# Projection pieces of an attention kernel, two chunks to a step in the narrow query blocks instead of one to a step throughout

## Chip, core and metric

The kernel runs on one NeuronCore of a Trainium2 chip. The metric is the device time of one execution in microseconds (us).

## What is computed

One layer of a language-model tower over 2 x 1024 tokens: a token embedding with two tables (hot and cold rows), causal attention with 16 heads of 32, and a mixture of experts. The part that matters here is the attention:

```python
qkv = jnp.einsum('bsd,od->bso', x, w_project)          # d = 512
q, k, v = (qkv[0], qkv[1], qkv[2])                     # 16 heads of 32
att = jnp.einsum('bhqd,bhkd->bhqk', q, k) / math.sqrt(HEAD_DIM)
att = jnp.where(causal[None, None, :, :], jnp.float32(-1000000000.0), att)
att = jax.nn.softmax(att, axis=-1)
out = jnp.einsum('bhqk,bhkd->bhqd', att, v)
```

## The kernel before

The program has three phases: tokens (until about 115 us of the profile), attention (to about 566 us), and output projection with the mixture of experts (the rest). Each engine runs a list of instructions written out by hand; semaphores tie the lists together.

**Units and steps.** Attention is cut into 8 units (u = 0 to 7), one for a group of 4 heads and one of the 2 sequences. A unit has 32 steps n: query block i = n // 4 (128 queries, i = 0 to 7) and head h = n % 4. Query block i looks at 128 (i + 1) keys, so steps 0 to 15 (blocks 0 to 3, "narrow") have up to 512 keys in one PSUM bank, and steps 16 to 31 (blocks 4 to 7, "wide") have up to 1024 keys in two. A step is a chain over four engines: PE multiplies the scores (L669), DVE finds the row maximum (`row_max`, L808), ACT takes the exponential (`exp`, L766), PE turns the probabilities 128 x 128 at a time (`turn`, L679), and ACT (L751) and DVE (L753) copy the turned banks out. Once in four steps, at n % 4 == 2, PE multiplies a finished block with v (`heads`, L692, and one transpose, L695), ACT copies the sums' inverses (L773) and DVE scales (L823). Scores are issued two steps ahead in the narrow half and one step ahead in the wide half.

**Fills.** While unit u runs, PE also projects q, k and v of unit u + 1 into bank 7. That is 6 fills f: q, k of the first 512 tokens (f = 0, 1), q, k of the second (2, 3), v of the first (4), v of the second (5). A fill is 4 pieces (`fill_piece`). A q or k piece is one chunk k of the 512 input features in three matmuls with high and low parts (L622); a v piece is one token tile in 4 products over all chunks (`value_products`, L635). Within a step, PE's order is scores, turn, fill piece, heads. After the last piece of a fill one engine copies bank 7 out (`fill_evac`): ACT for f = 0, 2 (L539) and 4 (L550), DVE for f = 1, 3 (L543) and 5 (L552). The next fill waits for that copy, since there is one bank for all. Before the change, piece k of fill f is at step 2 + 5 f + k and its copy-out at step 6 + 5 f:

```python
if nxt and 0 <= (n - 2) // 5 < FILLS and (n - 2) % 5 < KC:
    fill_piece(pe, u + 1, 1 - b, (n - 2) // 5, (n - 2) % 5, 16 * (g + 1 + b))
```

Unit 7 has no next unit and no fills.

**What hangs on a fill.** POOL splits the copied q and k into high and low parts (`split_part`, L474, L476), and splits the input rows of the next fills (`split_rows_in`, L497, L501), in the fixed order rows of the first half, q of the first half, rows of the second half, k, q, k (`att_pool`). SP then spreads the parts over partitions in 64 DMAs a unit (`stack_half`, L437): 32 once half of the running unit's scores are issued, and 32 once all are. The first score of a wide block (n = 16, issued in step 15) waits for the second 32.

Of the kernel before, what the change touches and what calls it, by code (L numbers as in the profile page):

```python
# [25 lines left out]
KC = D // P  # L26
# [18 lines left out]
SPLIT0 = 5  # L45
SLOT_RING = 6
SLOT0 = 6
PSLOTS = 2
ROUTED_RING = 8
X_RING = 16  # L50
# [16 lines left out]
def build(nc, a, out):  # L67
    ctx = ExitStack()
    with ctx:
# [312 lines left out]
        HEAD = 16  # L382
# [84 lines left out]
        def split_part(pool, u, side, half):  # L467

            c = slice(half * 512, half * 512 + 512)
            pool.wait_ge(s_fact if side == 0 else s_fdve, HEAD + 3 * u + half + 1)  # L470

            pool.wait_ge((s_high if half else s_low)[(u - 1) % 2], STACKED * ((u - 1) // 2 + 1))
            passed(pool)
            pool.tensor_copy(part_hi[:, side, c], full[:, side, :]).then_inc(s_hi, 1)  # L474
            pool.wait_ge(s_hi, HEAD + 4 * u + 2 * half + side + 1)
            pool.tensor_tensor(part_lo[:, side, c], full[:, side, :],  # L476
                               part_hi[:, side, c].bitcast(F32), ALU.subtract).then_inc(s_lo, 1)

        def split_rows_in(pool, u, half, c, part="both"):

            if u == 1 and half == 0:
                pool.wait_ge(s_xC, 12)
            elif u == 1 and c == 0:
                pool.wait_ge(s_xC, NT)
                pool.wait_ge(s_xpused, 1)
            else:
                v, p = (u, 1) if half else (u - 1, 3)
                if c < KC - 1:
                    pool.wait_ge(s_xpused, 6 * (u - 1) + 3 * half - 3 + c + 1)
                else:  # L490
                    pool.wait_ge(s_fill, HEAD + FILLS * v + p + 1)
# [11 lines left out]
        def split_weights_in(pool, u, c):  # L503

            g = u // 2
            if c == 0:
                pool.wait_ge(s_wq, 16 * (g + 1))
                if u >= 2:

                    pool.wait_ge(s_fill, HEAD + FILLS * (u - 1) + 4)  # L510
            src = w_unit[:, c, 0:2 * P]
            passed(pool)
            pool.tensor_copy(wq_hi[:, c, :], src).then_inc(s_wqhi, 1)
            pool.wait_ge(s_wqhi, 4 * g + c + 1)
            pool.tensor_tensor(wq_lo[:, c, :], src, wq_hi[:, c, :].bitcast(F32), ALU.subtract).then_inc(s_wqlo, 1)
# [15 lines left out]
        def fill_evac(eng, who, u, f, b):  # L531

            src = bank(7)
            n = HEAD + FILLS * u + f + 1
            if f in (0, 2) and who == "act":
                eng.wait_ge(s_fill, n)

# [70 lines left out]
        def fill_piece(pe, u, b, f, k, loads):  # L608

            if k == 0:  # L610

                if f >= 4:
                    pe.wait_ge(s_w, loads)
                copied, count = ((s_fdve, 0), (s_fact, 1), (s_fdve, 1), (s_fact, 2), (s_fdve, 2), (s_fact, 3))[f]
                pe.wait_ge(copied, HEAD + 3 * u + count)
            if f < 4:
                side, half = f % 2, f // 2
# [30 lines left out]
        def att_pe(pe):  # L648
# [49 lines left out]
            def unit(u, b, g, prev, nxt):  # L698

                for n in range(STEPS):  # L700
# [7 lines left out]
                        turn(u, n - 1)  # L708
                    elif prev:
                        turn(u - 1, STEPS - 1)  # L710
                    if nxt and 0 <= (n - 2) // 5 < FILLS and (n - 2) % 5 < KC:
                        fill_piece(pe, u + 1, 1 - b, (n - 2) // 5, (n - 2) % 5, 16 * (g + 1 + b))
                    if n % GH == 2:
                        if n > GH:
                            heads(u, b, n // GH - 1)
# [39 lines left out]
        def att_act(act):  # L755
# [19 lines left out]
            def unit(u, b, prev, nxt):  # L775
                for n in range(STEPS):
# [2 lines left out]
                    elif prev:  # L779
                        copy_turned(act, "act", u - 1, STEPS + n - 2)  # L780
                    exp(u, n)
                    if nxt and (n - 2) % 5 == 4 % 5 and 0 <= (n - 2) // 5 - 0 < FILLS:
                        fill_evac(act, "act", u + 1, (n - 2) // 5 - 0, 1 - b)
                    if n % GH == 3:
                        if n > GH:
                            z_row(u, n // GH - 1)
# [13 lines left out]
        def att_dve(dve):  # L800
# [24 lines left out]
            def unit(u, b, g, pg, nxt):  # L825

                for n in range(STEPS):
                    row_max(u, n)
                    if nxt and (n - 2) % 5 == 4 % 5 and 0 <= (n - 2) // 5 - 0 < FILLS:
                        fill_evac(dve, "dve", u + 1, (n - 2) // 5 - 0, 1 - b)  # L830
                    if n >= 2:
                        copy_turned(dve, "dve", u, n - 2)
                    elif pg is not None:
# [1120 lines left out]
```

## Time and profile before

| | us |
|---|---|
| median of 3 runs (lowest, highest) | 994.73 (993.75, 995.87) |
| the profiled execution's own time | 993.92 |
| its span | 992.1 |
| PE busy in the span | 916.0 (92%) |
| DVE, ACT, POOL busy | 662.9, 596.9, 430.9 |

The span is what the profile shows of one execution. Busy time says how much of the span an engine had an instruction in it; the ends of matmuls are modelled. The windows further below split one unit of the attention by the starts of ACT's exponential at the first step of each block (343.58 us is step 0 of unit 4, 366.04 us its step 16, 400.90 us step 0 of unit 5). All units with fills look alike: from 170.13, 228.10, 285.36, 343.58, 400.90 and 458.17 us the starts of units 1 to 6 are known, and 515.45 us starts unit 7.

### The profile page before, as it was taken

The page shows a single profiled execution, that of the slowest core. Times are in us where ns is not written, and L with a number is a line of the kernel's source. Part 1 is how long each engine was busy: PE and PEld are TensorE (multiplying, and loading weights), DVE is VectorE, ACT ScalarE, POOL GpSimd, SP SyncE. Part 2 cuts the span into 40 slices and gives each one's busy share as a digit, 9 for nine tenths or more (in the row PEclk, how much of TensorE's full clock was granted, in tenths as well). Part 3 has the DMA queues.
Part 4 walks back from the last instruction along what each step waited for, and adds up shares of the span by engine and source line. Part 5 has one row for each costly group of instructions (what it writes and reads, how often), then busy time and mean ns, then how long its engine had stood idle before and what let it go on. Part 6 is the DMA issues. An engine that isn't in the chain of part 4 may idle for free.

```text
span 992.1 us, 21913 instructions
## 1 busy us (share of the span) xinstructions
PE 916.0 (92%) x6923; PEld 701.3 (71%) x6923; DVE 662.9 (67%) x1746; ACT 596.9 (60%) x1306; POOL 430.9 (43%) x460
## 2 busy tenths in 40 slices
PE   6679899999999999999997999899989999999992
PEld 5335678787887878788785788777866666676661
DVE  8885667576666757566666676668866666666660
ACT  7222487777867777786778622221157777777770
POOL 2188554534515255441402126433263377346542
PEclk9699899999999999999999999999999999999997
DMA  6135442424324242432426131441469578746633
GB/s 225 37 93 129 133 118 54 96 57 108 86 65 100 50 117 48 102 82 65 97 46 216 51 119 63 156 195 43 181 214 376 121 134 213 232 86 116 94 53 43
DMA packets 60515, 114.46 MB, mean 115 GB/s; under 512 B 13492, under 2 KB 19636, under 8 KB 58098
## 3 DMA queue, kind: packets, MB, share of 16 engines
q1 hardware_dynamic: 48082, 87.15, 29.4%
q0 software_dynamic: 12320, 25.90, 13.9%
q8 instruction: 58, 0.95, 0.4%
q14 instruction: 55, 0.45, 0.2%
HBM read 53.03 MB, written 25.17 MB: 79 GB/s over the span
## 4 chain that ended last, share of the span: by engine, by line
PE 74%; DVE 10%; issue 5%; SPq 4%; ACT 3%; DMA 2%; POOL 1%; POOLq 0%; DVEq 0%; ACTq 0%
PE psum L1505 13%; PE psum L679 11%; PE psum L1580 8%; PE psum L692 6%; PE psum L669 6%; PE psum L622 6%; PE psum L635 5%; PE psum L644 4%; SPq L437 4%; PE psum L1435 3%; PE psum L1549 2%; PE psum L1527 2%; PE psum L601 1%; PE psum L695 1%; PE psum L1516 1%
## 5 line engine op out<-in xcount | busy, mean ns | idle before, releaser
L766 ACT ACTIVATE probs<-psum,nmax 128x128 f32<-128x128 f32 (+7 forms) x256 | 191.5, 748 | 37.2 <-DVE nmax L808 35.1
L808 DVE CUSTOM_DVE_ANT_0 psum<-psum,mask_row 128x128 f32<-128x128 f32 (+7 forms) x256 | 192.1, 767 | 28.0 <-PE psum L669 26.8
L679 PE MATMUL psum<-ident,probs 128*128 128x128 f32 x1152 | 175.0, 276 | 12.5 <-ACT probs L766 5.5
L679 PEld LDWEIGHTS psum<-ident,probs 128*128 128x128 f32 x1152 | 134.3, 140 | 48.1 <-ACT probs L766 18.0
L751 ACT COPY probsT<-psum 128x512 f32<-128x512 f32 (+3 forms) x256 | 129.6, 506 | 33.5 <-PE psum L679 31.1
L1042 POOL DMA_INDIRECT out<-xnT,slot_out x47 | 82.7, 1759 | 108.1 <-DMA out<-xnT,slot_out 70.3
L669 PE MATMUL psum<-k_low,q_stack 128*128 128x512 f32 (+2 forms) x256 | 105.1, 418 | 6.0 <-ACT probs L766 3.2
L474 POOL CAST part_hi<-full 128x512 fp32r<-128x512 f32 x28 | 17.1, 611 | 206.9 <-ACT full L539 161.1
L823 DVE TENSOR_TENSOR attnT<-psum,z_rows 128x128 f32<-128x128 f32 x64 | 18.7, 292 | 111.7 <-ACT z_rows L773 111.7
L1580 PE MATMUL psum<-w_dn,gated_T 128*128 x188 | 88.6, 593 | 1.0 <-ACT gated_T L1096 1.0
L1361 DVE TENSOR_TENSOR w_lo<-w_gu,w_hi 128x1024 fp32r<-128x1024 f32 x48 | 58.8, 1227 | 42.9 <-ACT w_hi L1125 40.3
L1361 DVE TENSOR_TENSOR ws_lo<-w_gu,ws_hi 128x1024 fp32r<-128x1024 f32 x46 | 56.3, 1227 | 36.0 <-ACT ws_hi L1125 33.8
L692 PE MATMUL psum<-probsT,v_unit 128*32 128x128 f32 x2304 | 76.2, 275 | 0.0
L501 POOL TENSOR_TENSOR x_lo<-xnT,x_hi 128x512 fp32r<-128x512 f32 x56 | 71.8, 1282 | 4.4
L692 PEld LDWEIGHTS psum<-probsT,v_unit 128*32 128x32 f32 x2304 | 59.0, 109 | 15.6 <-ACT probsT L751 7.8
L635 PE MATMUL psum<-w_unit,xnT 128*128 128x128 f32 x512 | 66.8, 275 | 0.2
L753 DVE COPY probsT<-psum 128x128 f32<-128x128 f32 (+3 forms) x128 | 62.2, 486 | 3.7 <-PE psum L679 2.9
L669 PEld LDWEIGHTS psum<-k_low,q_stack 128*128 128x128 f32 x256 | 51.9, 206 | 15.0 <-ACT probs L766 10.6
L635 PEld LDWEIGHTS psum<-w_unit,xnT 128*128 128x128 f32 x512 | 61.7, 192 | 0.6 <-issue 0.6
L1110 ACT ACTIVATE xnT<-psum,slot_w 128x512 f32<-128x512 f32 x47 | 32.4, 690 | 46.9 <-PE psum L1580 44.8
L1125 ACT CAST w_hi<-w_gu 128x1024 fp32r x48 | 50.3, 1049 | 10.8 <-issue 9.0
L622 PE MATMUL psum<-x_lo,wq_hi 128*128 128x512 f32 x112 | 53.8, 480 | 0.0
(262 smaller groups left out, 2144.5 us busy)
## 6 DMA issues: line engine op xcount, KB each, us to landing
w_gu<-in_wgu SPq DMA_DIRECT2D x16, 1024.0 KB, 7.9
q_stack<-part_hi SPq DMA_DIRECT2D x128, 64.0 KB, 2.0
q_stack<-part_lo SPq DMA_DIRECT2D x128, 64.0 KB, 2.0
w_dn<-in_wd SPq DMA_DIRECT2D x16, 512.0 KB, 9.2
out<-acc SPq DMA_DIRECT2D x17, 256.0 KB, 3.1
hot_all<-xn SPq DMA_DIRECT2D x4, 1024.0 KB, 8.0
h_scratch<-hot_all SPq DMA_DIRECT2D x16, 256.0 KB
k_low<-part_hi SPq DMA_DIRECT2D x64, 64.0 KB, 2.0
```

Of the source, the lines that this page charges most:

```text
L622: mm = pe.matmul(bank(7), w[:, k, side * P:(side + 1) * P], x[:, k, :], start=(k == 0 and t == 0), stop=(k == KC - 1 and t == 2), skip_gro ...
L635: mm = pe.matmul(bank(7)[:, k * P:(k + 1) * P], xnT[:, c, t0:t0 + P], w_unit[:, c, 2 * P:3 * P], start=(c == 0), stop=(c == KC - 1))
L669: mm = pe.matmul(dst[:, c0:c1], qs, ks[:, h, 0:c1 - c0], start=True, stop=True)
L679: mm = pe.transpose(bank(4 + m % 2)[:, (j - 4 * k) * P:(j - 4 * k + 1) * P], probs[n % PSLOTS][:, j * P:(j + 1) * P], ident[:, :])
L692: pe.matmul(bank(6)[32 * h:32 * h + 32, 0:P], v_unit[b][:, j, 32 * h:32 * h + 32], probsT[i % 2][:, h, j * P:(j + 1) * P], start=(j == 0), ...
L751: eng.copy(dst, src).then_inc(s_Ca, 1)
L766: act.activation(probs[n % PSLOTS][:, 0:(i + 1) * P], score_bank(n)[:, 0:(i + 1) * P], ACT.Exp, bias=nmax[:, n % 4:n % 4 + 1], scale=-1.0, ...
L808: dve.tensor_tensor_reduce(out=row, in0=row, in1=mask_row[:, (QT - 1 - i) * P:QT * P], scale=1.0, scalar=3.0e38, op0=ALU.add, op1=ALU.min, ...
L1042: pool.indirect_dma_start(out=out, out_offset=bass.IndirectOffsetOnAxis(ap=slot_out[:, j:j + 1], axis=0), in_=y_rows[j % ROUTED_RING], in_ ...
L1361: dve.tensor_tensor(w_lo[j % 2][:, k, :].rearrange("p k n -> p (k n)"), w_gu[:, bass.ds(slot, 1), k, :].rearrange("p o k n -> p (o k n)"), ...
L1505: mm = pe.matmul(bank(2 + p), x[:, p, k * P:(k + 1) * P], w[p][:, k, :], start=(k == 0 and t == 0), stop=(k == KC - 1 and t == 2), skip_gr ...
L1580: mm = pe.matmul(bank(6 + p), gated_T[:, p, k * P:(k + 1) * P], w_dn[:, bass.ds(half, 1), k, :].rearrange("p o n -> p (o n)"), start=(k == 0),
```

## The change

Fills and pieces are the same, but a table places them. The order of the fills becomes q, k, v of the first half, then q, k, v of the second. The first five fills have two pieces to a step, and start at steps 2, 5, 8, 11 and 14; the last v has one piece to a step, at 18 to 21. The copy-outs move to steps 4, 7, 10, 13, 16 and 22. The counts that other engines wait for follow the new order. POOL's and SP's lists are the same.

```diff
+FILL_ORDER = (0, 1, 4, 2, 3, 5)
+FILL_FROM = (2, 5, 8, 11, 14, 18)
+FILL_RATE = (2, 2, 2, 2, 2, 1)
...
-            pool.wait_ge(s_fact if side == 0 else s_fdve, HEAD + 3 * u + half + 1)
+            pool.wait_ge(s_fact if side == 0 else s_fdve, HEAD + 3 * u + (1, 3 - side)[half])
...
-                v, p = (u, 1) if half else (u - 1, 3)
+                v, p = (u, 1) if half else (u - 1, 4)
...
-                    pool.wait_ge(s_fill, HEAD + FILLS * (u - 1) + 4)
+                    pool.wait_ge(s_fill, HEAD + FILLS * (u - 1) + 5)
...
-            n = HEAD + FILLS * u + f + 1
+            n = HEAD + FILLS * u + FILL_ORDER.index(f) + 1
...
-                copied, count = ((s_fdve, 0), (s_fact, 1), (s_fdve, 1), (s_fact, 2), (s_fdve, 2), (s_fact, 3))[f]
+                copied, count = ((s_fdve, 0), (s_fact, 1), (s_fact, 2), (s_fact, 3), (s_fdve, 1), (s_fdve, 2))[f]
...
-                    if nxt and 0 <= (n - 2) // 5 < FILLS and (n - 2) % 5 < KC:
-                        fill_piece(pe, u + 1, 1 - b, (n - 2) // 5, (n - 2) % 5, 16 * (g + 1 + b))
+                    if nxt:
+                        for f, n0, rate in zip(FILL_ORDER, FILL_FROM, FILL_RATE):
+                            for k in range(KC):
+                                if n == n0 + k // rate:
+                                    fill_piece(pe, u + 1, 1 - b, f, k, 16 * (g + 1 + b))
...
-                    if nxt and (n - 2) % 5 == 4 % 5 and 0 <= (n - 2) // 5 - 0 < FILLS:
-                        fill_evac(act, "act", u + 1, (n - 2) // 5 - 0, 1 - b)
+                    if nxt:
+                        for f, n0, rate in zip(FILL_ORDER, FILL_FROM, FILL_RATE):
+                            if n == n0 + KC // rate:
+                                fill_evac(act, "act", u + 1, f, 1 - b)
```

DVE's list changes as ACT's does. Lines of the changed kernel are numbered a few higher (L622 is L625 there, L669 is L672, L679 is L682, L692 is L695).

PE's list in unit 1, steps 10 and 11 (a score L669, turns L679, a fill's chunk L622), before:

```order
L669 MATMUL psum<-k_low,q_stack 128x512
L679 MATMUL psum<-ident,probs 128x128 x3
L622 MATMUL psum<-x_lo,wq_hi 128x512
L622 MATMUL psum<-x_hi,wq_hi 128x512
L622 MATMUL psum<-x_hi,wq_lo 128x512
L692 MATMUL psum<-probsT,v_unit 32x128 x8
L695 MATMUL psum<-ident,z_inv 128x128
L669 MATMUL psum<-k_low,q_stack 128x512
L679 MATMUL psum<-ident,probs 128x128 x3
```

The same two steps of the changed kernel:

```order
L672 MATMUL psum<-k_low,q_stack 128x512
L682 MATMUL psum<-ident,probs 128x128 x3
L695 MATMUL psum<-probsT,v_unit 32x128 x8
L698 MATMUL psum<-ident,z_inv 128x128
L672 MATMUL psum<-k_low,q_stack 128x512
L682 MATMUL psum<-ident,probs 128x128 x3
L625 MATMUL psum<-x_lo,wq_hi 128x512
L625 MATMUL psum<-x_hi,wq_hi 128x512
L625 MATMUL psum<-x_hi,wq_lo 128x512
L625 MATMUL psum<-x_lo,wq_hi 128x512
L625 MATMUL psum<-x_hi,wq_hi 128x512
L625 MATMUL psum<-x_hi,wq_lo 128x512
```

Where one chunk stood in one step and none in the next, none stands now in step 10 and two behind each other in step 11. 

PE's list in unit 1, steps 28 and 29 (block 7, a value piece is L635), before:

```order
L669 MATMUL psum<-k_low,q_stack 128x512
L669 MATMUL psum<-k_high,q_stack 128x512
L679 MATMUL psum<-ident,probs 128x128 x7
L635 MATMUL psum<-w_unit,xnT 128x128 x4
L669 MATMUL psum<-k_low,q_stack 128x512
L669 MATMUL psum<-k_high,q_stack 128x512
L679 MATMUL psum<-ident,probs 128x128 x8
L635 MATMUL psum<-w_unit,xnT 128x128 x4
```

The same place of the changed kernel:

```order
L672 MATMUL psum<-k_low,q_stack 128x512
L672 MATMUL psum<-k_high,q_stack 128x512
L682 MATMUL psum<-ident,probs 128x128 x7
L672 MATMUL psum<-k_low,q_stack 128x512
L672 MATMUL psum<-k_high,q_stack 128x512
L682 MATMUL psum<-ident,probs 128x128 x8
```

Blocks 6 and 7 have no fill pieces left.

ACT's list in unit 1 around step 4 (the copy-out of the first fill is L539, now L542), changed kernel:

```order
L772 ACTIVATE probs,z_sum<-psum,nmax 128x256
L542 ACTIVATE full<-psum 128x512
L757 COPY probsT<-psum 128x128
L772 ACTIVATE probs,z_sum<-psum,nmax 128x256
L757 COPY probsT<-psum 128x256
```

The copy-out stood behind the exponential of step 6 and now stands behind that of step 4.

## Rows read from the trace of the kernel before

**Rows 1.** The page: span, busy time by engine, granted clock, chain by engine

```profile
span 992.1 us, 21913 instructions
...
PE 916.0 (92%) x6923; PEld 701.3 (71%) x6923; DVE 662.9 (67%) x1746; ACT 596.9 (60%) x1306; POOL 430.9 (43%) x460
...
PEclk9699899999999999999999999999999999999997
...
PE 74%; DVE 10%; issue 5%; SPq 4%; ACT 3%; DMA 2%; POOL 1%; POOLq 0%; DVEq 0%; ACTq 0%
```

**Rows 2.** Windows, unit 4: blocks 0 to 7, narrow half, wide half, last step

```profile
core 0: us, PE busy (x) PEld busy (x) DVE busy (x) ACT busy (x) POOL busy (x), PEclk, DMA share, GB/s
343.58:350.07 6.49, 5.94 (x89) 4.80 (x89) 3.14 (x14) 3.20 (x14) 0.00 (x0) 1.00 0.45 102
...
359.79:366.04 6.25, 5.95 (x53) 4.21 (x52) 3.90 (x11) 5.09 (x13) 4.45 (x5) 1.00 0.62 168
366.04:373.60 7.56, 7.44 (x71) 5.70 (x70) 4.44 (x13) 6.13 (x14) 1.89 (x2) 1.00 0.46 105
373.60:381.94 8.34, 8.15 (x93) 6.99 (x91) 6.08 (x17) 6.23 (x13) 5.49 (x8) 1.00 0.42 96
381.94:390.94 9.00, 9.00 (x111) 8.27 (x110) 6.97 (x16) 7.28 (x15) 8.00 (x11) 1.00 0.10 24
390.94:400.90 9.96, 9.96 (x124) 9.08 (x122) 7.41 (x17) 7.33 (x14) 0.00 (x0) 1.00 0.14 40
343.58:366.04 22.46, 21.61 (x213) 16.56 (x213) 13.05 (x48) 16.22 (x54) 11.10 (x12) 1.00 0.49 118
366.04:400.90 34.86, 34.55 (x390) 30.04 (x388) 24.90 (x60) 26.97 (x55) 15.38 (x20) 1.00 0.27 64
397.37:400.90 3.53, 3.53 (x72) 3.04 (x70) 1.89 (x6) 1.96 (x5) 0.00 (x0) 1.00 0.36 107
```

**Rows 3.** Windows, unit 7: narrow half, blocks 4 to 6, block 7's first three steps

```profile
515.45:535.24 19.79, 14.84 (x182) 11.00 (x181) 11.56 (x47) 15.17 (x54) 0.00 (x0) 1.00 0.43 97
535.24:541.61 6.37, 5.29 (x60) 3.83 (x59) 4.35 (x13) 5.64 (x15) 2.74 (x4) 1.00 0.97 375
541.61:549.31 7.70, 6.78 (x73) 4.83 (x74) 6.00 (x16) 6.08 (x13) 7.38 (x9) 1.00 0.84 297
549.31:557.64 8.33, 7.57 (x86) 5.47 (x86) 6.86 (x16) 6.58 (x13) 0.91 (x1) 1.00 0.19 63
557.64:562.95 5.31, 4.86 (x47) 3.34 (x49) 5.28 (x12) 4.97 (x9) 0.00 (x0) 1.00 0.00 0
```

**Rows 4.** Timeline of PE, unit 4, steps 3 to 4 (start, duration, instruction)

```profile
349.00 0.48 PE L622 MATMUL psum<-x_lo,wq_hi 128*128 128x512 f32 x1
...
349.78 0.28 PE L669 MATMUL psum<-k_low,q_stack 128*128 128x256 f32 x1
349.90 0.27 PE L679 MATMUL psum<-ident,probs 128*128 128x128 f32 x1
349.93 0.48 PE L622 MATMUL psum<-x_lo,wq_hi 128*128 128x512 f32 x1
```

**Rows 5.** Chain in order of time: a value piece, and twelve output-projection matmuls (start, length)

```profile
381.29 0.89 PE psum L635 x8
...
582.22 2.87 PE psum L644 x12
```

**Rows 6.** Sources L539 and L543: the copy-outs (min/median/max ns)

```profile
L539 ACT ACTIVATE full<-psum x14: 587/590/604, 121.3 to 481.4; 128x512 f32<-128x512 f32 x14
...
L543 DVE COPY full<-psum x14: 691/692/692, 126.9 to 489.8; 128x512 f32<-128x512 f32 x14
```

**Rows 7.** Timeline of POOL, unit 4: first row split after copy-out, last row split

```profile
352.82 0.61 POOL L474 CAST part_hi<-full 128x512 fp32r<-128x512 f32 x1 [24.41 <-ACT full L539]
...
361.19 1.28 POOL L501 TENSOR_TENSOR x_lo<-xnT,x_hi 128x512 fp32r<-128x512 f32 x1
```

**Rows 8.** Waits, the whole attention: scores that wait for stacks (us, times, longest)

```profile
PE psum L669 <- DMA k_high<-part_lo: 1.4, 2, 0.8
```

More of the change, by code:

```diff
@@ L828, in unit @@
                     row_max(u, n)
-                    if nxt and (n - 2) % 5 == 4 % 5 and 0 <= (n - 2) // 5 - 0 < FILLS:
-                        fill_evac(dve, "dve", u + 1, (n - 2) // 5 - 0, 1 - b)
+                    if nxt:
+                        for f, n0, rate in zip(FILL_ORDER, FILL_FROM, FILL_RATE):
+                            if n == n0 + KC // rate:
+                                fill_evac(dve, "dve", u + 1, f, 1 - b)
                     if n >= 2:
```

## The prediction

> **What bounds the kernel now.** I read the page first. PE is busy 92% of the span and holds 74% of the chain that ended last, at a granted clock that is full nearly everywhere [rows 1]. So the question is where PE has room, and I cut one unit of the attention into windows at ACT's exponentials of each block. In unit 4 PE is busy 21.61 of the 22.46 us of the narrow half and 34.55 of the 34.86 us of the wide half [rows 2]. A unit with fills is PE's from end to end, in both halves. What idle there is lies in block 0, 6.49 less 5.94, so 0.55, and in block 3, 6.25 less 5.95, so 0.30 [rows 2]. Block 0's idle is mostly the hand-over from the last wide block, ahead of the first fill.
>
> Unit 7 has no fills and shows the pace that the rest of a step sets. Its narrow half takes 19.79 us with PE busy 14.84, blocks 4, 5 and 6 take 6.37, 7.70 and 8.33 us with PE busy 5.29, 6.78 and 7.57, and the first three steps of block 7 take 5.31 us [rows 3]. So without fills the narrow half has 5 us of room on PE. But the fills before the change use up that room already.
>
> **What the change does.** No instruction is added or removed: 7 units have 16 q or k pieces and 8 v pieces each, before and after. Before, the narrow half holds 12 q or k pieces (steps 2 to 5, 7 to 10, 12 to 15) and the wide half 4 q or k and 8 v pieces. After, the narrow half holds 16 q or k and 4 v pieces, and the wide half 4 v pieces.
>
> *Price of a piece.* From step 3's chunk to step 4's chunk PE needs 0.93 us, of which the score takes 0.12 (349.78 to 349.90), and the turn that comes before the next chunk about 0.11. A chunk so costs 0.70 [rows 4]. A v piece costs 0.89 [rows 5]. Into the narrow half move 4 x 0.70 + 4 x 0.89 = 6.36 us per unit.
>
> *Do two chunks together cost less than two apart?* PE's rows give a chunk 0.78 us from its own start to the next score [rows 4], while twelve such matmuls in a row take 2.87 us, 0.24 each, so 0.72 for three [rows 5]. But the turn ahead of a chunk starts only 0.03 us before it [rows 4], so that the extra time is the turn's own. I take no gain. The Trainium skill (TensorE: Matmul & The Clock Gate, Step-by-step) says that a matmul alone cannot hide its drain and that in a stream the drain lies beneath the next one. Read as a price for each lone chunk, 0.78 less 0.70 over 8 pairs and 7 units, it would give back 4.5 us of the sum below; the saturated rows speak against it, as lone chunks there have other matmuls on both sides.
>
> *Narrow half.* PE is busy nearly throughout, so the 6.36 us are added. They can fill block 3's idle 0.30 and some of the modelled ends; I take off 0.5. What is new is that the copy-outs fall into short steps. From the end of a fill to the start of the next, PE has in between two steps' scores and turns. After the first fill that is about 0.12 + 0.11 + 0.12 + 0.22 = 0.57 us (two scores of 0.12, three turned tiles of 0.11 [rows 4]), while ACT's copy takes 0.59 [rows 6] and some 0.2 of signalling: 0.25 us of wait. After the other fills at least one block's heads or wider turns lie in between, and I price them at nothing; the heads cover them, and without them each costs up to what the first does. Behind the waiting chunk PE's queue holds the next score and turn, but DVE and ACT have a step in hand then. Narrow: 6.36 - 0.5 + 0.25 = +6.1 us per unit, 22.46 becomes 28.6. The bounds are all idle filled, 6.36 - 0.85 = +5.5, and four copy-outs fully exposed at 0.6 or 0.7 us each [rows 6] and 0.2 of signalling, 6.36 + 3.4 = +9.8.
>
> *Wide half.* PE's work there falls by 6.36 us, but the time cannot fall below the pace of unit 7. Block 6 goes from 9.00 to 8.33 [rows 2, 3]. In block 7 the first three steps go from 6.43 (9.96 less 3.53 [rows 2]) to 5.31 [rows 3], and the last step, where PE is busy all of 3.53 [rows 2], loses nearly its whole piece of 0.89, to 2.7: block 7 8.0. Blocks 4 and 5 take 15.90 us with the pieces of steps 17 to 20, 22 and 23, which are 4 x 0.70 + 2 x 0.89 = 4.58, and 14.07 without [rows 2, 3]; they keep 4 x 0.89 = 3.56. In proportion they would take 15.5, with PE saturated 15.90 - 1.02 = 14.9; I take 15.1, nearer to the saturated end, since PE is busy 15.59 of the 15.90 [rows 2]. Wide: 15.1 + 8.33 + 8.0 = 31.4, so -3.4 us per unit. The bounds are 15.5 + 8.33 + 8.2 = 32.0, -2.8, and unit 7's pace with no cost of the v pieces, 14.07 + 8.33 + 8.0 = 30.4, -4.5.
>
> What is late next in the wide half is ACT and DVE: the 3 us of PE work that do not come back as time turn into PE's waits for the exponential.
>
> *The copy-outs' engines.* ACT is busy 16.22 of 22.46 us in the narrow half and DVE 13.05 [rows 2]. One more copy on each (0.6 and 0.7 us) is hidden in the longer half.
>
> *POOL.* Its list is the same. The last x_lo of the second half ends 361.19 + 1.28 - 352.82 = 9.65 us after POOL takes up q [rows 7]. After the change q is copied out about 0.7 us sooner, and the fill that needs these rows starts at step 11 with two whole fills and their 6.36 us of PE between, some 10 us after that copy; its last chunk is read 1.5 us later still. Hidden, with 1 to 3 us to spare. Were it not, PE's whole list would stand behind that chunk.
>
> *SP.* Its 64 issues per unit stay. The second 32 have to land by step 15, and twice the scores waited for them, 1.4 us in all, 0.8 the longest [rows 8]; with DVE and ACT restarting behind, units 1 and 3 (170.13 to 228.10, 285.36 to 343.58) are 0.7 and 0.9 longer than unit 4. A narrow half that is 6 us longer hides that: -1.7 us in all. The first 32 and the loads of weights have more time than before.
>
> **The sum.** +6.1 - 3.4 = +2.7 us for each of 7 units, 18.9, less 1.7, is +17.2 us. Unit 7 and the phases before and behind stay. Against the profiled execution's own 993.92 us that is 1011.1; the median of the runs lies 0.8 above it, and so I predict 1012. A measurement of this kernel tells about 0.2%, 2 us, from no change.
>
> **Rivals.**
> - *Exposed copy-outs.* One PSUM bank serves all fills, so each of five fills in the narrow half has to be copied out before the next may start, 0.6 to 0.7 us and signalling each time. If the two steps between do not cover it, because a burst of 1.4 us on PE has starved DVE and ACT, all four cost 0.8: +9.8 - 3.1 = +6.7 per unit, +45 us, about 1040; half of that exposed gives 1028. For it: the first one has 0.57 us of PE work to hide 0.8. Against it: PE L622 shows no wait for a copy now, with the same distance of one step, and ACT is idle 28% of the narrow half [rows 2]. Chance 0.10, with what lies above 1024.
> - *The wide half pays everything back* (the other side). Unit 7's blocks 4 and 5 run beside weight loads of 375 and 297 GB/s [rows 3], where the units with fills have 105 and 96 [rows 2]. If unit 7's pace is set by that and not by the chain, the wide half stays PE-bound and loses its 6.36 us; the narrow half gains 5.5: -0.9 x 7 - 1.7 = -8 us, 987. It decides from a wide half below 29.4 us. Against it: block 6 of unit 7 has 63 GB/s and PE idle 0.76 of 8.33 us all the same, and DVE is busy 6.86 of it [rows 3]. Chance 0.04.
> - *A draw.* Wide half at the floor of 30.4 and narrow at +5.5: +1.0 x 7 - 1.7 = +5; with the lone-chunk gain of 4.5 it is nothing, 995. For it: each of the two bounds is possible alone. Chance 0.05.
> - The forecast with its bounds, 1002 to 1024: chance 0.81.
>
> **The numbers.** The range goes from 1002 (the two lower bounds: +5.5 - 4.5 = +1.0 and part of the way to the forecast) to 1024 (a third of the copy-outs' exposure). Slower by over 0.2%: 0.81 + 0.10 and a little of the draw, 0.92. Within 0.2%: 0.04. Faster: 0.04.
>
> **What would show it.** Right: unit 4's successor takes about 60 us from first exponential to first exponential (57.3 before), narrow 28.6 with PE busy nearly all of it, wide 31.4 with PE idle some 2 us or more; block 6 at 8.3; no DMA wait at step 15; the clock at 1.00. Wrong: a wide half below 30 us (rival two), a row of L625 or L638 with idle before it that ends with a copy-out at each fill (rival one), or POOL's x_lo as releaser of PE at step 11 or 12.

## The result and the profile after

The changed kernel takes 1021.43 us (median of 4 runs, 1019.97 to 1022.75) beside 994.81 us before: 1.0257 times as long, with a 95% interval of 1.0238 to 1.0276. It is 26.6 us slower. The profiled execution took 1022.02 us, with a span of 1020.2 us.

The page of the changed kernel, in the lines that answer to [rows 1]:

```profile
span 1020.2 us, 21913 instructions
...
PE 930.3 (91%) x6923; PEld 705.4 (69%) x6923; DVE 659.5 (65%) x1746; ACT 601.0 (59%) x1306; POOL 434.0 (43%) x460
...
PE 73%; DVE 10%; issue 6%; DMA 4%; ACT 3%; SPq 2%; POOL 1%; POOLq 0%; ACTq 0%; DVEq 0%
```

The page hardly differs: the same instructions, the same engine on the chain, 28.1 us more. PE is busy 14.3 us longer with the same 6923 matmuls, so its busy time, with modelled ends, is not a fixed sum of work. Windows tell more. Those of unit 4, cut at the same exponentials as in [rows 2] (blocks 0, 3, 4, 5, 6 and 7, then the narrow and the wide half; columns as there):

```profile
357.60:364.79 7.19, 6.64 (x91) 5.33 (x91) 3.15 (x14) 3.21 (x15) 0.00 (x0) 1.00 0.41 94
...
377.79:385.27 7.48, 7.48 (x63) 6.03 (x62) 3.39 (x10) 5.82 (x14) 1.91 (x2) 1.00 0.47 123
385.27:393.89 8.62, 7.56 (x81) 6.44 (x79) 5.02 (x15) 5.86 (x13) 6.58 (x10) 1.00 0.41 93
393.89:402.55 8.66, 8.20 (x93) 7.03 (x93) 6.88 (x17) 6.39 (x13) 6.91 (x9) 1.00 0.41 94
402.55:410.48 7.93, 7.35 (x86) 5.49 (x86) 6.50 (x16) 6.59 (x13) 0.00 (x0) 1.00 0.19 50
410.48:418.46 7.98, 7.53 (x95) 5.63 (x93) 6.40 (x16) 6.94 (x14) 0.00 (x0) 1.00 0.13 29
357.60:385.27 27.67, 27.00 (x254) 22.15 (x254) 12.90 (x47) 17.89 (x56) 12.95 (x14) 1.00 0.44 104
385.27:418.46 33.19, 30.63 (x349) 24.59 (x347) 24.80 (x61) 25.78 (x53) 13.49 (x18) 1.00 0.29 68
```

The narrow half went from 22.46 to 27.67 us, with PE busy nearly throughout, and the wide half from 34.86 to 33.19 with PE idle 2.56. Blocks 6 and 7, without pieces, fell to 7.93 and 7.98. Block 4 rose from 7.56 to 8.62 and block 5 from 8.34 to 8.66, though block 4 holds about as much fill work as before (two thirds of a chunk and two v pieces, against three chunks) and block 5 one chunk less.

Where PE's idle time in block 4 comes from, in the timeline of the changed kernel (start, duration, instruction, idle before and its releaser):

```profile
385.60 0.39 PE L625 MATMUL psum<-x_hi,wq_lo 128*128 128x512 f32 x1
...
386.02 0.69 DVE L546 COPY full<-psum 128x512 f32<-128x512 f32 x1 [0.78 <-PE psum L625]
...
386.63 0.17 DVE L823 RECIPROCAL z_rec<-z_sum 128x4 f32<-128x4 f32 x1
386.83 0.23 DVE L825 COPY z_inv<-z_rec 128x128 f32<-128x128 f32 x1
386.98 0.82 DVE L816 CUSTOM_DVE_ANT_0 psum<-psum,mask_row 128x640 f32<-128x640 f32 x1
...
387.89 0.80 ACT L772 ACTIVATE probs<-psum,nmax 128x640 f32<-128x640 f32 x1 [0.50 <-DVE nmax L816]
...
388.83 0.50 PE L672 MATMUL psum<-k_low,q_stack 128*128 128x512 f32 x1 [1.06 <-ACT probs L772]
```

The second chunk of step 15 ends, DVE has waited 0.78 us for it, copies k out, inverts the sums and only then takes the row maximum of step 17. The exponential and the score two steps on wait behind it, and PE stands idle for 1.06 us.

Step by step, the 28.1 us between the two spans: unit 0 starts 0.87 later (116.37 for 115.50), units 0 to 6 take 423.90 us for 399.95, which is 23.95 more, and from the start of unit 7 to the end it is 479.93 for 476.65, 3.28 more. Of these 3.28, unit 7 has 1.26: from its first exponential to the end of its last it takes 49.88 us for 48.62. The other 2.0 fall behind it, where the edit touches nothing; over all kernels below that stretch runs from 426.5 to 431.2 us (428.0 before, 430.1 here). Unit 7 has a new wait, in PE's timeline of the changed kernel:

```profile
559.73 0.48 PE L672 MATMUL psum<-k_low,q_stack 128*128 128x512 f32 x1 [1.79 <-DMA k_high<-part_lo]
...
560.92 0.78 PE L672 MATMUL psum<-k_low,q_stack 128*128 128x512 f32 x1
```

and in the windows of its narrow half and its block 4 the granted clock is no longer 1.00:

```profile
540.27:561.79 21.52, 15.35 (x179) 11.46 (x179) 11.79 (x48) 15.18 (x53) 0.00 (x0) 0.96 0.44 98
561.79:569.51 7.72, 7.05 (x66) 5.11 (x64) 5.24 (x15) 6.88 (x17) 4.63 (x6) 0.89 1.02 394
```

The narrow half of unit 7 takes 21.52 us where it took 19.79 [rows 3]. The stacks are issued once all scores of unit 6 are out. Unit 6's last step is now 2.66 instead of 3.53 us [rows 2], so the stacks start about 0.9 us later against unit 7, and unit 7 has no fills that would hide them. The last part of k_high lands 19.32 us after the first exponential of unit 7, before the change 18.11 us after it. That the shorter last step is what makes this difference is argued; no run varied it.

### The profile page after: what moved, and what is told of

The parts are those of the page before. It is cut to its first block, busy times and chain, and to the rows that moved or that the text cites. A ratio compares the mean times of both kernels' runs of the same rounds, so it can differ in the third digit from the quotient of the medians.

```text
span 1020.2 us, 21913 instructions
## 1 busy us (share of the span) xinstructions
PE 930.3 (91%) x6923; PEld 705.4 (69%) x6923; DVE 659.5 (65%) x1746; ACT 601.0 (59%) x1306; POOL 434.0 (43%) x460
## 4 chain that ended last, share of the span: by engine, by line
PE 73%; DVE 10%; issue 6%; DMA 4%; ACT 3%; SPq 2%; POOL 1%; POOLq 0%; ACTq 0%; DVEq 0%
PE psum L682 12%; PE psum L1515 11%; PE psum L625 8%; PE psum L672 7%; PE psum L1590 7%; PE psum L695 7%; PE psum L638 5%; PE psum L647 4%; DMA out<-xnT,slot_out 4%; PE psum L1445 3%; SPq L440 2%; PE psum L1559 2%; PE psum L1537 2%; PE psum L698 2%; DVE oh_lo L1756 1%
## 5 line engine op out<-in xcount | busy, mean ns | idle before, releaser
L816 DVE CUSTOM_DVE_ANT_0 psum<-psum,mask_row 128x128 f32<-128x128 f32 (+7 forms) x256 | 192.1, 767 | 25.7 <-PE psum L672 23.8
L682 PE MATMUL psum<-ident,probs 128*128 128x128 f32 x1152 | 175.2, 278 | 12.1 <-ACT probs L772 4.2
L682 PEld LDWEIGHTS psum<-ident,probs 128*128 128x128 f32 x1152 | 132.7, 141 | 48.9 <-issue 23.3
L672 PE MATMUL psum<-k_low,q_stack 128*128 128x512 f32 (+2 forms) x256 | 108.7, 437 | 18.7 <-ACT probs L772 16.3
L477 POOL CAST part_hi<-full 128x512 fp32r<-128x512 f32 x28 | 17.2, 614 | 224.3 <-ACT full L542 197.6
L695 PE MATMUL psum<-probsT,v_unit 128*32 128x128 f32 x2304 | 76.2, 275 | 0.0
L672 PEld LDWEIGHTS psum<-k_low,q_stack 128*128 128x128 f32 x256 | 52.1, 207 | 30.9 <-ACT probs L772 26.3
L695 PEld LDWEIGHTS psum<-probsT,v_unit 128*32 128x32 f32 x2304 | 59.0, 109 | 14.5 <-issue 11.8
L638 PE MATMUL psum<-w_unit,xnT 128*128 128x128 f32 x512 | 64.5, 275 | 0.2
L1135 ACT CAST ws_hi<-w_gu 128x1024 fp32r x46 | 48.3, 1051 | 9.7 <-issue 6.5
```

The costliest lines, as they stand in the source:

```text
L638: mm = pe.matmul(bank(7)[:, k * P:(k + 1) * P], xnT[:, c, t0:t0 + P], w_unit[:, c, 2 * P:3 * P], start=(c == 0), stop=(c == KC - 1))
L672: mm = pe.matmul(dst[:, c0:c1], qs, ks[:, h, 0:c1 - c0], start=True, stop=True)
L682: mm = pe.transpose(bank(4 + m % 2)[:, (j - 4 * k) * P:(j - 4 * k + 1) * P], probs[n % PSLOTS][:, j * P:(j + 1) * P], ident[:, :])
L695: pe.matmul(bank(6)[32 * h:32 * h + 32, 0:P], v_unit[b][:, j, 32 * h:32 * h + 32], probsT[i % 2][:, h, j * P:(j + 1) * P], start=(j == 0), ...
L816: dve.tensor_tensor_reduce(out=row, in0=row, in1=mask_row[:, (QT - 1 - i) * P:QT * P], scale=1.0, scalar=3.0e38, op0=ALU.add, op1=ALU.min, ...
L1135: act.copy(w_hi[j % 2][:, k, :].rearrange("p k n -> p (k n)"), w_gu[:, bass.ds(slot, 1), k, :].rearrange("p o k n -> p (o k n)")).then_inc ...
```

## The experiments

Units tell more than one whole execution does: within one trace they agree to 0.2 us wherever no DMA wait or POOL work falls on them, while the phases before and behind move by 1 to 2 us and more between executions (unit 0 starts between 114.90 and 116.51 us over these kernels, though none touches what lies ahead of it). So for each kernel the narrow and the wide half of a unit stand beside the time. All were run once and profiled, apart from c2. Kernel before, in the same sessions: 997.61 us (e1 to e4), 996.14 (e5 to e7, b1), 995.86 (c1 to c4); times of one session compare best.

| kernel | what it is | time, us | unit | narrow | wide |
|---|---|---|---|---|---|
| before | | 994.8 | 57.32 | 22.46 | 34.86 |
| changed | | 1021.4 | 60.86 | 27.67 | 33.19 |
| e1 | new order, one piece a step | 996.20 | 57.49 | 22.64 | 34.85 |
| e2 | e1 with double steps | 1028.98 | 62.31 | 24.52 | 37.79 |
| e3 | changed, k copy-out at 17 | 1015.64 | 60.27 | 27.69 | 32.58 |
| e4 | old order, v in the wide half | 1042.71 | 63.95 | 29.27 | 34.68 |
| e5 | e3, v copy-out at 31 | 1014.97 | 59.72 | 27.69 | 32.03 |
| e6 | e4 with a gap at 8 to 10 | 1023.45 | 61.16 | 26.06 | 35.10 |
| e7 | changed, products left out | 968.22 | 53.17 | 22.80 | 30.37 |
| b1 | before, all a step earlier | 1008.86 | 59.04 | 22.99 | 36.05 |
| c1 | e3, last v at 19 to 22 | 1015.08 | 59.73 | 27.70 | 32.03 |
| c2 | before, f 2 double, f 3 at 15 | 996.11 | 57.35 | 23.00 | 34.35 |
| c3 | before, f 2 double | 996.91 | 57.57 | 23.01 | 34.56 |
| c4 | before, f 4 double | 1000.65 | 58.20 | 22.43 | 35.77 |

(Unit 4 for the first rows to e4 and for e7, unit 6 for e5, e6, b1 and c1 to c4. In some kernels the units differ: units 2 and 4 of e5 and c1 take 60.0 us, units 1 to 5 of b1 59.3 to 59.7, units 1, 3 and 5 of c2 57.6 to 57.7, units 1 to 6 of e4 63.0 to 64.5 and of e7 53.2 to 55.0.)

### Order and bursts apart: e1 and e2

```diff
-FILL_FROM = (2, 5, 8, 11, 14, 18)
-FILL_RATE = (2, 2, 2, 2, 2, 1)
+FILL_FROM = (2, 7, 12, 17, 22, 27)
+FILL_RATE = (1, 1, 1, 1, 1, 1)   # e1
+FILL_RATE = (2, 2, 2, 2, 2, 2)   # e2
```

> The new order of the fills (q, k, v of the first half, then q, k, v of the second), one piece to a step as before, starts at steps 2, 7, 12, 17, 22, 27. Theory 1 (moving PE work into the narrow half is what costs): the narrow half gets 4 v pieces for 4 q pieces, 4 x 0.19 = +0.8 us of PE work, the wide half loses it, so a unit takes 57.3 plus 0 to 0.5 us and the kernel 994 to 999. Theory 2 (two pieces on one step starve DVE and ACT, the copy-outs are exposed): there are no double steps, a unit takes 57.3, the kernel 994 to 996. Theory 3 (the order itself makes POOL late: the second k is copied out at step 26 and the next unit's splits start 5 steps later): PE L625 waits at steps 2 to 5 for x_lo, 1 to 3 us in every second unit, 997 to 1005.

> As e1, but two pieces to a step: steps 2-3, 7-8, 12-13, 17-18, 22-23, 27-28. The narrow half has the same 12 pieces as in e1, so only the bursts differ. Theory 1: within 0.5 us per unit of e1, since PE is the bound in both. Theory 2: 1 to 3 us per unit more than e1, half or more of the changed kernel's 3.5, that is 7 to 20 us on the kernel.

Windows of unit 4, narrow and wide half, e1:

```profile
343.39:366.03 22.64, 22.09 (x233) 18.05 (x232) 13.06 (x48) 16.21 (x54) 11.06 (x12) 1.00 0.48 118
366.03:400.88 34.85, 34.01 (x372) 28.78 (x370) 24.65 (x60) 26.80 (x55) 15.44 (x20) 1.00 0.27 64
```

and e2:

```profile
362.89:387.41 24.52, 23.20 (x238) 18.88 (x237) 12.65 (x48) 16.78 (x55) 11.18 (x12) 1.00 0.48 116
387.41:425.20 37.79, 34.47 (x363) 27.96 (x363) 25.07 (x60) 26.19 (x54) 15.38 (x20) 1.00 0.25 59
```

The order alone costs 0.17 us per unit: theory 3 (POOL late) falls, and no L625 waits for x_lo in e1. The same pieces in the same halves in pairs (two pieces in one step, a burst) cost 1.9 us in the narrow and 2.9 in the wide half, and the kernel 32.8 us, more than the 7 to 20 expected. Theory 1 in the form of this expectation, PE's sum and nothing else, falls for pairs: in the wide half PE is idle 3.3 of 37.79 us. e2 also leaves three steps empty behind each fill and puts DVE's copy-outs in the wide half at steps 24 and 29, so bursts, empty steps and copy-outs are not yet apart.

### One burst at a time: c3 and c4

```diff
+FILL_FROM = (2, 7, 12, 17, 22, 27)
+FILL_RATE = (1, 1, 2, 1, 1, 1)   # c3, on the kernel before
+FILL_RATE = (1, 1, 1, 1, 2, 1)   # c4, on the kernel before
```

> The kernel before with one edit: the second q in two double steps at 12 and 13 (narrow half), copy-out at 14; all else in place. Theory 1 (in the narrow half scores are two steps ahead, so a burst is absorbed and only PE's sum counts): block 3 stays at 6.3 plus 0 to 0.3, unit 57.3 to 57.6, kernel 995 to 997. Theory E (a burst costs by itself): 0.7 or more per unit, kernel 1000 or more.

> The kernel before with one edit: the first v in two double steps at 22 and 23 (wide half), ACT's copy-out at 24 instead of 26; all else in place. Theory E/2 (in the wide half scores are one step ahead, so that a burst of 1.78 us delays the next score and DVE and ACT run dry, and the steps freed of pieces, 24 and 25, fall only to DVE's pace): +0.7 to +1.5 us per unit, kernel 1000 to 1006. Theory 1 (PE's sum alone): 57.3 plus 0.3 at most, kernel 995 to 997.

Windows of unit 6, c3's halves:

```profile
458.98:481.99 23.01, 22.16 (x218) 17.27 (x217) 13.00 (x48) 16.65 (x56) 12.98 (x14) 1.00 0.41 94
481.99:516.55 34.56, 33.42 (x383) 29.65 (x383) 24.50 (x60) 26.55 (x53) 1.88 (x2) 1.00 0.28 63
```

the last chunk of the pair in c3's step 13 of unit 6:

```profile
477.95 0.47 PE L624 MATMUL psum<-x_lo,wq_hi 128*128 128x512 f32 x1 [0.28 <-POOL x_lo L503]
```

and c4's wide half and block 5:

```profile
486.17:521.94 35.77, 35.09 (x390) 29.91 (x388) 24.51 (x61) 26.98 (x54) 3.78 (x4) 1.00 0.26 59
493.73:502.97 9.24, 9.05 (x100) 7.89 (x99) 6.09 (x17) 6.24 (x14) 1.88 (x2) 1.00 0.44 101
```

One fill in double steps costs 0.3 us per unit in the narrow half (57.57 for 57.28 in the same unit of before) and 0.9 in the wide half. In c3 the narrow half grows by 0.6 us and block 4, which has lost ACT's copy-out to step 14, shrinks by 0.3. PE waits there for POOL's x_lo once in each unit, 7 times and 1.9 us in all, as the line shows; the kernel before has no such wait. Its 0.28 us is as large as the whole cost, so c3 does not show that the burst itself costs anything; in the changed kernel, where the first v stands between, no L625 waits for x_lo.

In c4 block 5 takes 9.24 for 8.34, since it holds the third v piece that block 6 held before, and block 6 stays at 9.0 though its first two steps are free of pieces now.

Both forecasts of the unit and kernel time held, theory 1's for the narrow half and theory E/2's for the wide half; block 3 of c3 took 6.87 us, not the 6.3 to 6.6 expected. That the difference comes from the look-ahead, two steps or one, is argued, since it was never varied. The two fills also differ in size (0.70 and 0.89 us a piece), and c4 moves ACT's copy-out from step 26 to 24, where DVE inverts the sums. Three fills in double steps at 0.9 would make 2.7 of e2's 2.9 us, but e2 moves DVE's copy-outs too, and how its 2.9 divides was not tried.

### The copy-outs in the wide half: e3, e5, c1

```diff
-                            if n == n0 + KC // rate:
+                            if n == n0 + KC // rate + (f == 3):                        # e3, c1
+                            if n == (31 if f == 5 else n0 + KC // rate + (f == 3)):    # e5
-FILL_FROM = (2, 5, 8, 11, 14, 18)
+FILL_FROM = (2, 5, 8, 11, 14, 19)                                                      # c1
```

> The changed kernel with one thing moved: the copy-out of the second k (DVE) stands at step 17 behind that step's row maximum, not at step 16 ahead of it. The next fill starts at step 18, as before. Theory 1 (PE throughput alone): block 4 stays at 8.62 us, kernel 1021. Theory 2 (in the wide half, where scores are one step ahead, DVE's 0.69 us copy and its wait of 0.78 for the burst's end stand ahead of the row maximum of step 17, and PE then idles 1.06 us for an exponential): the interval from step 16 to 17 falls from 2.62 to about 1.9, block 4 to about 8.0, 0.5 to 0.8 us per unit, kernel 1016 to 1018.

> As e3, and the copy-out of the second v (DVE) stands at step 31 instead of step 22; no fill follows it within the unit. Theory A (a DVE copy of 0.69 us in the wide half delays the row maximum, the exponential and so PE, because scores are one step ahead there): the interval from step 22 to 23 falls from 2.48 to about 1.5, block 5 from 8.66 to 7.7, block 7 rises by 0 to 0.7, so 0.3 to 0.9 us per unit less than e3, kernel 1009 to 1014. Theory B (the 4 v pieces are what makes block 5 longer): block 5 stays at 8.66, kernel 1015 to 1016.

> As e3 (copy-out of the second k at step 17), and the last v fill starts at step 19 instead of 18, so that its DVE copy-out stands at step 23, where PE is in the heads of step 22. Theory A (what a DVE copy-out costs in the wide half depends on its step: dear at n % 4 == 0, where DVE also inverts the sums, cheap at n % 4 == 3, where PE is in the heads): block 5 falls from 8.66 to about 8.1 as with e5, where the copy went to the unit's end, and nothing rises in blocks 6 and 7: a unit 59.5 to 59.9, kernel 1012 to 1015. Theory B (every DVE copy-out in the wide half costs its 0.69): 60.3 as e3.

Block 4 of unit 4 in e3, block 5 of unit 6 in e5 and block 5 of unit 6 in c1:

```profile
382.17:390.19 8.02, 7.56 (x81) 6.44 (x79) 4.90 (x14) 5.78 (x14) 5.06 (x7) 1.00 0.44 101
```

```profile
508.45:516.55 8.10, 7.97 (x93) 7.04 (x93) 5.58 (x16) 6.58 (x13) 0.00 (x0) 1.00 0.43 100
```

```profile
506.43:515.43 9.00, 8.87 (x101) 7.99 (x101) 6.33 (x17) 6.58 (x13) 0.00 (x0) 1.00 0.46 104
```

One DVE copy moved by one step takes block 4 from 8.62 to 8.02 us, with PE busy the same 7.56 us in both, and 0.6 off the unit. The other one, moved from step 22 to the unit's end, takes block 5 from 8.66 to 8.10. c1 moves a v piece into block 5 and the copy from step 22 to step 23: block 5 takes 9.00, but block 4 gave 0.9 back (7.12), and the unit is as short as e5's, 59.73. So the two copy-outs cost 0.6 and 0.55 us per unit more where the change puts them than at step 17 and at the unit's end or step 23; that they cost nothing there was not tried. In the units theory A held and theory B fell.

The kernel times show less. e3's 1015.64 us lie just below theory 2's 1016 to 1018, and c1's 1015.08 just above its 1012 to 1015. e5 missed theory A's 1009 to 1014 with 1014.97 and is 0.67 us below e3. Units 0 to 6 of e5 take 2.8 us less than e3's (block 6 gives 0.3 back in units 0, 2 and 4, see the last section), and from the start of unit 7 to the end it takes 2.2 more, of which 1.9 lie behind the last exponential, where e5 and e3 are the same. Over units 0 to 6, e5 takes 7.4 us less than the changed kernel and c1 7.5.

My guess in c1's expectation of 8.1 us for block 5 was wrong by the v piece that moved there. What makes step 23 cheap, PE's heads of step 22, is argued; only the position was varied.

### POOL and the fill between: e4 and e6

```diff
+FILL_FROM = (2, 5, 8, 11, 18, 24)    # e4, on the kernel before, order q k q k v v
+FILL_FROM = (2, 5, 11, 14, 18, 24)   # e6
+FILL_RATE = (2, 2, 2, 2, 1, 1)
```

> The old order q, k, q, k, v, v with double steps for q and k (2-3, 5-6, 8-9, 11-12) and the two v fills back in the wide half with one piece to a step (18 to 21, 24 to 27). Narrow half 16 x 0.70 = 11.2 us of pieces, against 8.4 before and 14.8 in the changed kernel; the wide half keeps 7.1. Theory 1: in proportion to the PE work that moves, 2.8 of 6.36: narrow about 22.46 + 2.3 = 24.8, wide about 34.86 - 1.0 to -2.0, so +0.3 to +1.5 us per unit, kernel 997 to 1005. Theory 2: four bursts and three copy-outs in the narrow half as in the changed kernel, +2.5 or more per unit, kernel 1012 to 1020.

> As e4 (old order, both v fills in the wide half, q and k in double steps), but the second q and k at steps 11-12 and 14-15, where the changed kernel has them, with nothing at steps 8 and 9. In e4 PE waited 0.55 us and more for POOL's x_lo at the second q's chunks, and with it for what stands behind. Theory C (the first v between k and q is what covers POOL's row splits of 4 x 1.93 us): without the v but with the gap the waits for x_lo vanish; narrow about 24.5, wide about 34 to 35, a unit 59 to 60, kernel 1006 to 1014. Theory D (bursts cost by themselves, wherever POOL is): narrow 27 or more, kernel above 1020.

Timeline of e4, PE at step 8 and POOL's split of the rows (L624 is the chunk, L503 x_lo):

```profile
383.50 1.29 POOL L503 TENSOR_TENSOR x_lo<-xnT,x_hi 128x512 fp32r<-128x512 f32 x1
...
384.94 0.47 PE L624 MATMUL psum<-x_lo,wq_hi 128*128 128x512 f32 x1 [0.55 <-POOL x_lo L503]
```

Windows of e6's unit 6, narrow and wide:

```profile
481.17:507.23 26.06, 23.88 (x222) 18.53 (x222) 12.87 (x47) 17.12 (x55) 13.02 (x14) 1.00 0.39 89
507.23:542.33 35.10, 32.90 (x381) 28.46 (x379) 24.29 (x61) 26.56 (x53) 1.89 (x2) 1.00 0.26 60
```

Neither theory stated for e4 was right: it is 45 us slower than before. The second q at step 8 needs rows that POOL has not split, a wait I had put into no expectation; PE waited for x_lo 21 times, 13.9 us in all, and e4's block 2 takes 8.4 us. With a gap in place of the pieces (e6) block 2 takes 5.08 and the waits are gone. In the changed kernel the first v stands where e6 has the gap, and gives POOL the same time. That it is needed there follows from e4 and e6; it was not tried in the changed order. But e6 is no better than the change (61.16 us). Its narrow half takes 3.6 us more than before for 2.8 us more of pieces, with PE idle 2.2; its wide half keeps both v fills and a DVE copy-out at steps 16 and 28. Theory C's waits vanished, but its time of 1006 to 1014 was missed; the 1023.45 us lie in theory D's range, above 1020, and its narrow half of 27 or more did not come. So neither theory holds whole.

### Is the narrow half PE's? e7

```diff
-                for t, (w, x) in enumerate(((wq_hi, x_lo), (wq_hi, x_hi), (wq_lo, x_hi))):
+                for t, (w, x) in enumerate(((wq_lo, x_hi),)):
...
-            for c in range(KC):
+            for c in range(cs):        # cs = 1 in the fills
```

> The changed kernel with one of three matmuls of each q or k chunk and one of four products of each v piece left out of none but done alone: two thirds of the q and k products and three quarters of the v products are left out, all waits, copies and DMAs stay. PE's fill work falls from 18.3 to 5.5 us per unit. Theory 1 (PE throughput bounds the narrow half): narrow 27.7 falls to 21 to 22, where the stacks (24.7 us from SP's first issue to landing) begin to bound it; the wide half falls by less, to about 31. Unit 52 to 54, kernel 958 to 975. Theory 2 (copy-outs and their steps bound the narrow half): narrow stays above 25, kernel above 985.

```profile
328.97:351.77 22.80, 19.42 (x206) 14.57 (x205) 13.37 (x48) 16.96 (x56) 12.95 (x14) 1.00 0.50 116
351.77:382.14 30.37, 27.72 (x318) 20.81 (x316) 23.98 (x61) 25.43 (x53) 13.53 (x18) 1.00 0.34 79
```

With 5.5 us of fill work in place of 18.3 (estimates, from the prediction's prices of a piece) the narrow half falls by 4.9 us and the wide half by 2.8. Theory 2 falls. Theory 1 holds for the kernel time, with a floor a little above its 21 to 22 for the narrow half: in this faster kernel PE waits for POOL's x_lo at one chunk in each unit (9.1 us over 7), which the changed kernel does not. So of the change's 27.67 us the work on PE makes at least 4.9, and what is left, this new wait included, takes 22.8, no better than the whole narrow half of the kernel before with 12 pieces in it.

### Tries for a better version: b1 and c2

```diff
+FILL_FROM = (1, 6, 11, 16, 21, 26)    # b1, on the kernel before, one piece a step
+FILL_FROM = (2, 7, 12, 15, 22, 27)    # c2, on the kernel before
+FILL_RATE = (1, 1, 2, 1, 1, 1)        # c2
```

> The kernel before with every fill one step earlier (1, 6, 11, 16, 21, 26; copy-outs at 5, 10, 15, 20, 25, 30), one piece to a step. PE idles about 1 us between step 30 and step 2, and the first piece can fill part of it; the last piece leaves step 30, whose interval carries heads and a piece. If unit time is PE's work plus its idle (54.3 + 3.0), 0 to 0.6 us per unit less, 991 to 995 beside 995 of before. If DVE's copies at 10 and 30 hurt more than at 11 and 31, up to 0.5 us per unit more, 998.

> The kernel before with the second q in two double steps (12, 13; copy-out at 14) and the second k two steps earlier (15 to 18; DVE copy-out at 19, beside heads, not 21). Theory A: the 0.68 us of step 21 go (2.04 to about 1.4), the double steps cost up to 0.4 in block 3: 56.8 to 57.4 per unit, kernel 991 to 996. Theory E (a double step costs about 0.7 wherever it is): 57.7 or more, 998 or more.

b1 is 12.7 us slower than the kernel before beside it, outside both expectations. Block 5 takes 9.20 for 8.34: its DVE copy-out now stands at step 20, a step in which DVE also inverts the sums. That this is the reason, and how the 2.0 us per unit divide (413.72 for 399.95 over units 0 to 6), was not tried.

c2 is the same as before: 996.11 us, median of 10 runs, beside 995.86 of 13, 1.0007 times with an interval of 0.9994 to 1.002; units 0 to 6 take 399.81 us for 399.95. Block 5 of unit 6 fell by 0.36 us (7.98 for 8.34), with the copy-out at step 19 and one chunk less in it, which are not apart here. Block 3 rose by 0.6, with the wait for x_lo of c3 in it (7 times, 1.9 us in all). No version here beats the kernel before.

## Why the prediction was right, and where it was off

The direction was right, and so was the main mechanism: PE's work is added to the narrow half in full, and the wide half gives only a part back. The forecast was 1012 in a range of 1002 to 1024, and the time is 1021.4: +26.6 us where +17.2 was forecast. The sum was short by a third. In the two traces, 28.1 us apart, the 10.9 beyond the forecast are 6.7 in units 0 to 6, 1.3 in unit 7 and 2.9 ahead of and behind the attention, where nothing was changed.

**The price of a piece and what moves.** The 0.70 us of a chunk held, and the lone-chunk gain that I refused is not there: in the changed kernel's timeline six matmuls of a double step follow each other at the same 0.23 us as three did.

```profile
363.72 0.48 PE L625 MATMUL psum<-x_lo,wq_hi 128*128 128x512 f32 x1
364.03 0.40 PE L625 MATMUL psum<-x_hi,wq_hi 128*128 128x512 f32 x1
364.26 0.39 PE L625 MATMUL psum<-x_hi,wq_lo 128*128 128x512 f32 x1
364.50 0.39 PE L625 MATMUL psum<-x_lo,wq_hi 128*128 128x512 f32 x1
364.72 0.39 PE L625 MATMUL psum<-x_hi,wq_hi 128*128 128x512 f32 x1
364.95 0.39 PE L625 MATMUL psum<-x_hi,wq_lo 128*128 128x512 f32 x1
365.18 0.28 PE L672 MATMUL psum<-k_low,q_stack 128*128 128x256 f32 x1
```

Step 3 with its two chunks takes from 363.72 to 365.18, 1.46 us, against 0.78 for the one [rows 4], or 0.73 each. The first matmul takes 0.31 to the next and the others 0.23. That extra 0.08 is no saving of pairs: in a step without a chunk the first score behind the turn has it instead (0.32 from 386.52 to 386.84, where a score behind a chunk takes 0.23, from 385.82 to 386.05). The Trainium skill (TensorE: Matmul & The Clock Gate, Step-by-step), read as a price for each lone chunk, would have put the total 4.5 us below my sum. The trace does not bear that reading out, and the total came out above.

**Narrow half.** +6.1 forecast, +5.2 measured. Most of the difference is bookkeeping: the pair of chunks in step 15 ends 0.55 us after the exponential of step 16 has begun (385.82 and 385.27), and counts in the wide half's window so far, where the single chunk before ended 0.13 us ahead of it. The wait behind the first copy-out is there, at 0.36 us instead of 0.25 (PE's weights L625 wait 7 times for ACT's copy, 2.5 us in all). No run shows the 0.2 of signalling in that term as such: PE's weights start 0.05 us behind the copy.

**Wide half: the step that failed.** -3.4 forecast, -1.7 measured. Blocks 6 and 7 came to 7.93 and 7.98, against 8.33 and 8.0 in the sum. Blocks 4 and 5 came to 17.28 instead of 15.1. Of these 2.2 us, about 0.7 is the shift of the pair just named, 0.6 is DVE's copy-out at step 16 (e3) and 0.55 the one at step 22 (e5, c1). Under "the copy-outs' engines" I had weighed only the two copies that join the narrow half, and called them hidden since ACT and DVE have idle time there. I did not look at where the other two land. In a half where DVE is busy 24.9 of 34.86 us a copy of 0.69 seems free too; e3 shows that it is not, and that its place in DVE's queue ahead of the next row maximum is what costs. That this needs scores only one step ahead is argued. An engine's idle share does not tell it. About 0.35 of the 2.2 us stay open.

**Unit 7 "stays": failed.** It went from 48.62 to 49.88 us, first exponential to end of the last. The wait for the stacks (1.79 us) is the new thing in it, with the lower clock behind it; block 6 gave 0.4 back (7.93 for 8.33). The relief in units 1 and 3, forecast at 1.7 us (0.7 and 0.9 make 1.6), came: no other unit waits for k_high any more. But I sized the stacks' slack only for the units with fills.

**The rivals.** Exposed copy-outs was the nearest, but not by its own mechanism: it had PE wait for the bank after each fill, and PE did so only once per unit, 0.36 us. What the copy-outs cost came by DVE's queue in the wide half, about 1.15 us per unit by block 4 of e3 and block 5 of e5, and 7.4 us over units 0 to 6 of e5. The wide half paying everything back did not happen: PE idles 2.56 us in it. That unit 7's pace was set by something beside the chain was partly so (last section), worth 0.4 us in block 6. POOL was rightly priced at nothing in the changed kernel, and e4 shows how near that was.

## What to carry to other kernels

A piece of filler work has two prices, the time it takes on the bound engine and what the copy-out behind it does to another engine's queue; read the second from the step it lands in, not from that engine's busy share. A burst of filler is not dear or cheap by itself: one fill in double steps cost 0.3 us in a half with scores two steps ahead, a wait for another engine's input included, and 0.9 in a half with one step ahead. Look which wait it brings before blaming the burst. When a unit without filler is used as the floor, look for what else runs beside it, and ask what its own hidden transfers need once its neighbours end sooner.

## What the runs showed that I had not expected

**A DVE copy held up by POOL.** In e5 and c1 block 6 took 8.21 to 8.25 us in units 0, 2 and 4 and 7.93 in the others. In c1's unit 4 POOL splits rows at that time, in unit 5 it does not:

```profile
394.44 1.09 DVE L816 CUSTOM_DVE_ANT_0 psum<-psum,mask_row 128x896 f32<-128x896 f32 x1
395.18 1.27 POOL L504 TENSOR_TENSOR x_lo<-xnT,x_hi 128x512 fp32r<-128x512 f32 x1
...
395.99 0.55 DVE L825 COPY z_inv<-z_rec 128x128 f32<-128x128 f32 x1
...
456.07 0.23 DVE L825 COPY z_inv<-z_rec 128x128 f32<-128x128 f32 x1
456.21 1.09 DVE L816 CUSTOM_DVE_ANT_0 psum<-psum,mask_row 128x896 f32<-128x896 f32 x1
```

The small copy between two SBUF tiles takes 0.23 us alone and 0.55 beside the POOL instruction, and ends 0.09 us behind it. Over the changed kernel its durations run from 0.226 to 0.958:

```profile
L825 DVE COPY z_inv<-z_rec x64: 226/226/958, 118.8 to 593.7; 128x128 f32<-128x128 f32 x64
```

In the 14 traces 261 of these copies took over 0.3 us, and each of them ended 0.08 or 0.09 us behind a POOL instruction that was under way when it started. The row maximum L816, which works on PSUM, takes 1.09 us beside POOL (394.44) and 1.09 without it (456.21). The Trainium skill (SBUF — State Buffer, Who interferes with whom) describes a pair of SBUF ports that VectorE and GpSimd take by an exclusive lock, held for a whole instruction; the same page (SBUF: two separate sides) names an fp32 copy from SBUF to SBUF as one of VectorE's operations that wants it. The traces agree with that.

In unit 7 of the kernel before, a floor of the prediction [rows 3], the copies at the start of blocks 5 and 6 took 0.83 and 0.62 us beside POOL, and the blocks 7.70 and 8.33, where unit 7 of the changed kernel has 7.31 and 7.93. The overlap was not varied there. A long copy need not cost time: at the start of block 5 of the changed kernel it takes 0.96 us in units 0, 2 and 4 and 0.57 in 1, 3 and 5, and the block 8.66 in all.

**The clock after a short gap.** In unit 7 of the changed kernel PE does nothing from about 557.9 to 559.7 us, and matmuls of 512 columns then take 0.78 us where 0.48 is usual:

```profile
557.94:559.73 1.79, 0.00 (x2) 0.03 (x1) 0.29 (x1) 0.71 (x3) 0.00 (x0) 1.00 0.32 73
560.05:563.46 3.41, 3.41 (x14) 2.84 (x13) 2.04 (x6) 2.04 (x5) 0.00 (x0) 0.50 0.80 262
```

The granted clock is 0.50, the lower level of 1.2 GHz, from 560.05 to 563.46 us, and 1.00, 2.4 GHz, before and behind. In unit 7 of the kernel before PE's longest gap was 1.1 us, and the clock stayed at 1.00 [rows 3]. In the other kernels it fell in unit 7 behind waits of 2.0 to 2.6 us (e3, e4, e5, c1) and not behind 1.1 to 1.4 (b1, e2, e6, e7). The length of the last gap does not settle it alone: four times within e4's units (145.85 us is one) and twice in e7's it fell too, though PE had no gap above 1.3 us there, and those kernels have the same gaps in units where it did not fall.

**The price of a burst in the wide half.** The prediction had no term for it. At 0.9 us for each fill in double steps (c4) it would have been a large one, had the change doubled its pieces there too.
